# Masks of the merged diagonal maxima: added by VectorE in PSUM instead of by TensorE products

## What is computed

```python
scores = jnp.einsum('bhqd,bhkd->bhqk', q, k) / math.sqrt(HEAD_DIM)
causal = jnp.tril(jnp.ones((seq_len, seq_len), dtype=bool))
scores = jnp.where(causal[None, None, :, :], scores, jnp.float32(-1e+20))
attn = jax.nn.softmax(scores, axis=-1)
out = jnp.einsum('bhqk,bhkd->bhqd', attn, v)
```

## Time and profile before

| what | us |
|---|---|
| median of 3 runs | 3376.62 (3371.54 to 3381.6) |
| the profiled execution | 3371.2 |
| its span, first to last instruction | 3369.4 |
| TensorE busy | 3236.2 (96%) |
| VectorE busy | 2391.3 (71%) |
| GpSimd busy | 2245.7 (67%) |
| ScalarE busy | 1423.1 (42%) |

### The profile page before, as it was taken

One profiled execution on the slowest core, in us unless ns is written; L12 is line 12 of the kernel. 1 busy time (PEld: TensorE's weight loads), 2 busy tenths in 40 slices (PEclk: granted clock), 3 DMA queues, 4 the chain that ended last, 5 costly groups with the idle time before them and its releaser, 6 DMA issues. The chain is left out here.

```text
span 3369.4 us, 59196 instructions
## 1 busy us (share of the span) xinstructions
PE 3236.2 (96%) x23824; PEld 2288.1 (68%) x23824; DVE 2391.3 (71%) x4362; ACT 1423.1 (42%) x1679; POOL 2245.7 (67%) x1033
## 2 busy tenths in 40 slices
PE   1899999999999999999999999999999899999999
PEld 1778888846666666666666666666665688888887
DVE  3667777678888888888888888888883544444443
ACT  2222222235665666666566656656656200100110
POOL 3443330049999999999999999999998222332331
PEclk8999999989999999999999999999999999999999
DMA  9999994561221222122122212212221343433342
GB/s 240 242 253 230 233 234 147 147 198 42 68 63 38 63 65 59 43 73 63 43 58 66 54 43 69 57 43 55 60 57 35 120 95 96 93 86 100 92 90 63
DMA packets 248270, 335.04 MB, mean 99 GB/s; under 512 B 64371, under 2 KB 153715, under 8 KB 247995
## 3 DMA queue, kind: packets, MB, share of 16 engines
q1 hardware_dynamic: 229562, 264.13, 29.0%
q0 software_dynamic: 18432, 67.12, 9.3%
HBM read 227.73 MB, written 101.71 MB: 98 GB/s over the span
## 5 line engine op out<-in xcount | busy, mean ns | idle before, releaser
L932 ACT ACTIVATE probs<-st_ps 128x1024 f32<-128x1024 f32 (+1 forms) x1152 | 1066.5, 974 | 673.4 <-PE st_ps L1097 447.2
L984 DVE TENSOR_REDUCE mpart<-mx_ps 128x1 f32<-128x512 f32 (+2 forms) x1728 | 1092.0, 683 | 196.8 <-PE mx_ps L1058 132.3
L1058 PE MATMUL mx_ps<-k_max,qs 96*128 96x512 f32 (+3 forms) x2560 | 844.2, 399 | 9.8 <-DVE mpart L984 3.2
L1097 PE MATMUL st_ps<-qs,k_score 98*128 98x512 f32 (+1 forms) x2304 | 668.3, 390 | 0.0
L1058 PEld LDWEIGHTS mx_ps<-k_max,qs 96*128 96x128 f32 x2560 | 438.8, 190 | 315.5 <-DVE mpart L984 162.3
L901 POOL TENSOR_TENSOR sums<-sums,probs 128x1024 f32<-128x1024 f32 x252 | 607.4, 2410 | 20.5 <-ACT probs L932 0.8
L899 POOL TENSOR_TENSOR sums<-probs 128x1024 f32<-128x1024 f32 x252 | 601.4, 2386 | 17.4 <-ACT probs L932 12.9
L1113 PE MATMUL od_ps<-probs,vs 128*32 128x256 f32 (+1 forms) x9216 | 589.4, 373 | 1.4 <-ACT od_sb L939 1.4
L907 POOL TENSOR_TENSOR sums<-sums,probs 128x1024 f32<-128x1024 f32 (+1 forms) x252 | 531.4, 2109 | 19.8
L1097 PEld LDWEIGHTS st_ps<-qs,k_score 98*128 98x128 f32 x2304 | 421.0, 190 | 99.2 <-ACT probs L932 24.0
L1301 POOL TENSOR_TENSOR h<-h,bb 128x1024 f32<-128x1024 f32 x32 | 104.2, 3257 | 509.5 <-DVE xn_c L1375 509.5
(11 more groups left out here) (117 smaller groups left out, 3991.4 us busy)
## 6 DMA issues: line engine op xcount, KB each, us to landing
qs<-q_hi_scratch SPq DMA_DIRECT2D x128, 256.0 KB, 4.7
h_scratch<-hbuf SPq DMA_DIRECT2D x32, 512.0 KB, 4.4
q_hi_scratch<-rot_hi SPq DMA_DIRECT2D x64, 256.0 KB
q_lo_scratch<-rot_lo SPq DMA_DIRECT2D x64, 256.0 KB
qs<-q_lo_scratch SPq DMA_DIRECT2D x64, 256.0 KB, 5.9
o_scratch<-od_sb SPq DMA_DIRECT2D x128, 128.0 KB
o_in<-o_scratch SPq DMA_DIRECT2D x32, 512.0 KB, 4.9
o_in<-recip_scratch SPq DMA_DIRECT2D x128, 128.0 KB, 8.0
```

Of the source, the lines that this page charges most:

```text
L932: nc.scalar.activation(probs[:, n % SLOTS, half, :, lo:QW], st_ps[:, half, :, lo:QW], ACT.Exp, scale=float(HD) ** -0.5).then_inc(exp_done, 1)
L984: nc.vector.tensor_reduce(mpart[:, rows, kc], scored, AX, ALU.max).then_inc(max_done, 1)
L1058: mm = nc.tensor.matmul(out[:, j], qs[c][0:K_ROWS, h, t * P:(t + 1) * P], k_max[0:K_ROWS, kc * CT:kc * CT + w], start=j == 0, stop=late or ...
L1097: mm = nc.tensor.matmul(out[:, :, lo:QW], k_score[0:M_ROW + 2, kt * P:(kt + 1) * P], qs[c // 2][0:M_ROW + 2, h:h + 2, at + lo:at + QW], st ...
```

## The change

TensorE no longer makes the mask product of a merged unit; its bank is complete with the last head's product. VectorE adds the mask to the last 128 columns of each head in PSUM, waits for its own addition through a new semaphore, and then reduces as before. In `max_entries` a merged unit now has a weight of 1.9 (four heads) or 1.5 (two heads) instead of 1.0, which moves the places of units among the steps.

```diff
+def masked_together(unit):
+
+    c, kc, t, heads = unit
+    return kc == c and len(heads) > 1
+
...
+MERGED = [n for n, u in enumerate(MAXES) if masked_together(u)]
...
-    work = [(1.25 if u[2] == 3 else 1.05) if masked_late(u) else 1.0 for u in MAXES]
+    work = [(1.25 if u[2] == 3 else 1.05) if masked_late(u) else
+            (1.9 if u[2] == 0 else 1.5) if masked_together(u) else 1.0 for u in MAXES]
...
                 else:
+                    if kc == c:
+                        over = masks[:, 5:6, :].broadcast_to([P, len(heads), P])
+                        nc.vector.tensor_tensor(scored[:, :, w - P:w], scored[:, :, w - P:w], over, ALU.add
+                                                ).then_inc(max_masked, 1)
+                        dve.wait_ge(max_masked, g * len(MERGED) + MERGED.index(unit) + 1)
                     nc.vector.tensor_reduce(mpart[:, rows, kc], scored, AX, ALU.max).then_inc(max_done, 1)
...
-                diagonal, late = kc == c, masked_late(MAXES[unit])
+                diagonal = kc == c
...
-                                          k_max[0:K_ROWS, kc * CT:kc * CT + w], start=j == 0, stop=late or not diagonal)
-                if diagonal and not late:
-                    over = mqk.rearrange("p (h w) -> p h w", h=1).broadcast_to([P, many, P])
-                    mm = nc.tensor.matmul(out[:, :, w - P:w], ident_m, over, start=False, stop=True)
+                                          k_max[0:K_ROWS, kc * CT:kc * CT + w], start=j == 0, stop=j == many - 1)
                 mm.then_inc(max_ready, 1)
```

More of the change, by code:

```diff
@@ L666, in part_b @@
         od_sb = sb("od_sb", [P, 2, 2, QW], F32)
-        ident_m, mqk = masks[:, 0, :], masks[:, 5, :]
         mkq = masks[:, 1:2, :].broadcast_to([P, GROUP, P])
@@ L687, in part_b @@
         max_ready, max_done, max_all = sem("max_ready"), sem("max_done"), sem("max_all")
+        max_masked = sem("max_masked")
         m_hi_done, m_rows = sem("m_hi_done"), sem("m_rows")
```

## The result

The changed kernel takes 3426.62 us (median of 4 runs, 3423.81 to 3427.14) against 3374.44 us for the kernel before in the same measurement: a ratio of 1.015, interval 1.0136 to 1.0165. It is 52 us slower where 1 us less was forecast, and outside the range of 3364 to 3396. The profiled execution took 3427.1 us, with a span of 3425.3.

What follows compares the result with a forecast made beforehand. GpSimd and TensorE were taken to need equal time per group, with GpSimd the next floor. + 3 us at the start and - 4 in six groups gave - 1: 3375.6 us against 3376.62, range 3364 to 3396.

Steps and rivals of the forecast that it cites:

- What bounds the kernel: Attention groups: GpSimd and TensorE take about the same time; GpSimd needs 117.75 us in groups 2 to 9, else 117.0.
- The first rival: TensorE alone sets the time, so its 30 us come off: 3350 us with no stalls; chance 0.10.
- TensorE's saving of 1.9 us per group: TensorE loses 192 mask products, at 0.23 or 0.12 us each: 30 us in all.
- The price of an addition: Mask additions on VectorE take 697 or about 430 ns, costing 0.73 or 0.46 us: 6.6 us per group, 106 in all.
- New stalls of 0.8 us per group: TensorE waits longer at diagonal steps because VectorE's additions delay what is queued behind; bounds 0 and 6.6 us.
- The two places I named: Score masks of step 0, a stall of 0.4 to 0.6 us, and of step 15, 0.2 to 0.3.
- the next maxima: Maxima queued behind each merged unit: TensorE can be three banks ahead, so half a microsecond of delay is absorbed.
- The spread weights: New weights move 1 to 2 units to neighbouring steps, claimed to change no sum.
- Does the added work lengthen GpSimd's?: GpSimd's additions beside the new VectorE ones, which have one SBUF operand: no lengthening, 2.38 us as before.
- The start: Opening of the attention part, where VectorE is the bound: + 3 us, bounds 0 and 5.
- the 33 us I had looked at: From 727 to 760 us, VectorE busy 29.6 of 33 us: + 0.8 us, bounds 0 and 1.65.
- The second one: VectorE comes too late at the masks of steps 0 and 15: 118.7 us per group, 3396 us; chance 0.28.

Runs made afterwards that it cites:

- the version of three four-head units: Kernel before, with masks on VectorE for three of four four-head units (not step 19's), old weights, subtractions behind steps 17 and 18: 3367.49 us, ratio 0.9955.
- the run without masks: Kernel before with the mask products of the merged maxima left out and put nowhere, and the subtractions replaced by memsets: 3360.72 us, ratio 0.9949.
- the run with the same weights: Kernel before, masks on TensorE, with the new weights and the subtractions behind steps 17 and 18: 3382.70 us, ratio 1.0027.

## Why the prediction was wrong, point by point

*What bounds the kernel.* Right. GpSimd's 117.0 and 117.75 us per group are the floor: 116.9 were measured where TensorE was made faster than that, and 117.67 with the subtractions in the version of three four-head units. The first rival (TensorE decides alone) is refuted by the run without masks.

*TensorE's saving of 1.9 us per group.* Right as a size: without masks the steps with merged units are 1.8 us shorter together (14, 15, 19, 25, 35, 0 and the light step 18), of which 0.9 go into a wait for GpSimd in step 2 (4.22 us against 3.30).

*The price of an addition.* Right: 695 and 422 ns, 34 ns to the reduction. VectorE's busy time per group rose by 5.1 us (from 100.1 in group 14 to 105.2 in group 11 after) where 6.6 were reckoned: the sum left out that an addition can begin before the instruction ahead of it ends (by 0.09 us at 2086.47). The 101 us given beside it for 0.70 and 0.43 us is 100.

*New stalls of 0.8 us per group.* Mis-sized. In the same spread, masks on TensorE and on VectorE give the same 118.4 us; since 1.8 to 1.9 us of products are gone, the new stalls are 1.8 to 1.9. The two places I named show 0.7 us (step 1, 3.36 against 2.68 in the run with the same weights) and 0.4 us (step 16, 3.41 against 2.99), near or a little over my 0.4 to 0.6 and 0.2 to 0.3. The rest is spread over steps 15, 20 and 26, which I had let pass because "the next maxima" would absorb it. The stall I should have counted is that of VectorE's backlog as such, not that at one mask.

*The spread weights, "which changes no sum".* Wrong: + 0.5 us per group by themselves, 8 us over 15 groups. The steps differ by up to 0.75 us both ways as units move. In step 22 TensorE now waits 0.23 us for VectorE, in place of 0.10 us in step 29; what makes up the rest of the 0.5 was not settled.

*"Does the added work lengthen GpSimd's?"* This is the step that failed. I read the row of 2.70 against 2.38 us as VectorE holding GpSimd, asked whether the new additions would do it too, and answered rightly no. The other direction I left at nothing, though the row of 1.28 us for L1017, whose least duration was 0.68, shows it: GpSimd holds VectorE. How long depends on when in an addition the subtraction arrives: for the first subtraction of a group 0 in the kernel before and 2 us in the changed one. A shift of 0.27 us against GpSimd was enough. With the clock that fell behind it and the second subtraction, it cost 2.4 to 6.0 us in each of the eight groups against 118.4, 35 of the 52 us. The Trainium skill states it in the section I had cited ("SBUF — State Buffer", "Who interferes with whom"): the order of issue decides which of the two is blocked. The runs agree: 2.71 us when VectorE came 0.22 us after GpSimd, 0.68 when it came first.

Which part of the change shifted the arrival no run separates, but the traces with the subtractions at steps 17 and 18 allow an estimate. In group 6 VectorE ends the maxima of step 12, behind which the subtraction would stand, at 41.56 us with the new weights alone, 0.29 us after GpSimd's addition began (41.27). With the additions alone and the old weights it ends them at 41.77, 0.08 after (41.69). Since the subtraction begins 0.08 us before their end in both kernels, it would come 0.2 us into the addition in the first case and with its start in the second: by this estimate the new spread made the shift, the term that "changes no sum".

*The clock.* Not in the prediction. The earlier trace rows had it at 1.00 in the groups shown. Behind the stalls it came down to 0.57 over 4 us, which cost 1.6 us in most of the eight groups. The cause stays open: the run with the first subtraction of the kernel before at step 13 had two holds in each group (its steps 14 and 15 were longer by 1.3 and 1.0 us) and kept its clock.

*The start.* 3.2 us up to the first scores, 2.1 forecast: near. Group 0: 3.8 us instead of 0.8. There the maxima run with a third more units per step, VectorE is the bound for longer than the 33 us I had looked at, and with the masks on TensorE and the new weights the group has 127.3 us. The clock differs too: 0.93 in the mean of this group, against 0.96 before and in that run. How much of the missing 3.0 us it explains was not separated.

*The rivals.* The second one had the sign, the starving of GpSimd through ScalarE, and the test that was written for it (periods over 118 us, GpSimd waiting for ScalarE) came true. But it put all of it on score masks in steps 0 and 15 and ended at 3396; with the hold out of the way the kernel is at 3389.5. That this lies near 3396 is in part luck: the rival had 0.95 us per group, all from the additions, and of the 0.6 measured 0.5 come from the new weights. The missing 37 us belong to a mechanism that no rival named. The range was bounded by costs that I had added up from the new instructions; it did not contain what a shift in time does to old ones.

## What to carry to other kernels

An engine at 86% busy whose queue holds an instruction that another engine can lock out has no fixed price for that instruction: look at the spread between its least and its mean duration, and ask for each change that shifts its start, by as little as 0.3 us here, what it will meet. Put such instructions where the engine's delay stops nobody (here four and five steps later, worth 37 us in the changed kernel), before weighing anything else. And when work is moved from one engine to another, count the receiving engine's backlog at its densest step against the buffers in between: 0.12 or 0.23 us of work saved on TensorE was not worth 0.46 or 0.73 us on VectorE, except in the steps with room.

## What the runs showed of the hardware that I had not expected

- A subtraction on VectorE with two SBUF operands took 0.68, 1.28, 1.47, 2.08 or 2.7 us for the same 512 elements, by where in GpSimd's addition of 2.38 us it arrived. A held one always ended 0.55 us after that addition. GpSimd's own addition that followed the hold, or began just after the subtraction, took 2.69 to 2.94 us instead of 2.385.
- The granted clock fell from 1.00 to half for 3.4 us behind two stalls of about 1.4 us, at steps 13 and 15, in the middle of a stage that was otherwise busy over 97%. With one such stall it fell in two of seven groups. In one group of the changed kernel, and in all eight groups of the run with steps 14 and 15 longer by 1.3 and 1.0 us, it did not fall.
- Memsets of 512 elements (0.485 us each) in place of the two subtractions still cost 0.5 us per group in the changed kernel.
